# Expert tiles of 128 rows in place of 256, six weight buffers, and a semaphore for each weight matrix

## The chip, the core and the metric

The kernel runs on one core of one Trainium2 chip. The metric is the time of one execution on the device, in microseconds (us). The core has five engines that run side by side and wait for each other through semaphores: TensorE (PE: matrix products into the accumulation memory PSUM; PEld is its stream of weight loads), VectorE (DVE), ScalarE (ACT), GpSimd (POOL) and SyncE (SP). SP and POOL issue the DMAs; 16 DMA engines carry them out.

## What is computed

Two blocks of a gated cross-attention model over x (8 x 512 rows of 256). The change touches only the last step, a layer of eight experts, of which each of the 4096 rows uses one:

```
logits = x_flat @ w_gate + b_gate
route_idx = argmax(softmax(logits))            # one expert of 8 for each row
route_p = max(softmax(logits))
h = relu(x_flat @ W1[e] + b1[e])               # W1[e]: 256 x 1024
y = h @ W2[e] + b2[e]                          # W2[e]: 1024 x 256
x = x + tanh(g_ffn[1]) * y[route_idx] * route_p
```

Everything is float32. One expert's two matrices hold 1 MiB each.

## The kernel before

For some 2940 us the kernel works through the eight batch elements: three attention layers, whose units are interleaved on the engines by tables of numbers (`U_...`), and at the end of each element a normalised row, a residual row and the row's gate weight are stored to DRAM (`dramR`, 528 floats for each row). None of that is touched by the change, apart from two constant ramps.

Then comes the expert stage. The rows are sorted by expert on the device: VectorE ranks them, counts the rows of each expert and splits each expert's rows into tiles of TS = 256 rows. Since the number of rows of an expert is not known when the program is built, ET = 4096 / 256 + 7 = 23 tiles always run; `tex[j]` holds tile j's expert, and `idg` the row numbers that tile j gathers, in pieces of 128 (NH = 2 pieces for a tile). For each tile j:

- SP, `load_weights(j)` (L511 to L523), reads the expert's number and issues four DMAs: W1, b1, W2 and b2 (b2 repeated for 128 partitions). There are two buffers, and one semaphore for each buffer, `w_loaded[par]`, that counts all four. Tile j waits for `v_y`, VectorE's count of finished pieces, to show tile j-2 done.
- POOL, `fetch(j)` (L677), gathers NH pieces of 128 rows from `dramR` into `xs`, XB = 3 tiles ahead; `give_back(j)` (L686) scatters the results to `dramO`.
- TensorE: `turn_rows(j)` (L1326) turns the tile's rows with KD x NH = 4 transposes; `hidden(j)` (L1338) makes 8 x 2 products with a 128x128 block of W1 as the weights and the TS turned rows as the moving columns; `outputs(j)` (L1349) makes, for each of NH pieces, 8 products with 128 rows of `hT` as the weights and 256 columns of W2 moving. A float32 product is two instructions in the trace, so hidden and outputs have 32 each for a tile. The order is hidden(j), turn_rows(j+1), outputs(j).
- ScalarE, `hidden(j)` (L877), applies bias and relu, 8 operations of 128 x TS for a tile, from PSUM to `hT`.
- VectorE, `rows_in(j)` (L1813), copies the turned rows to SBUF; `rows_out(j)` (L1817) adds b2, scales and adds the residual, two operations for a piece.

After the last piece has been scattered, SP copies `dramO` to the output in eight DMAs (L533).

Of the kernel before, what the change touches and what calls it, by code (L numbers as in the profile page):

```python
# [8 lines left out]
F32 = mybir.dt.float32  # L9
# [3 lines left out]
ALU = mybir.AluOpType  # L13
# [3 lines left out]
B, S, C, D = 8, 512, 1601, 256  # L17
P = 128
QT = S // P
KD = D // P  # L20
# [22 lines left out]
NE, FF = 8, 1024  # L43
FM = FF // P
TOK = B * S
NT = TOK // P
TS = 256
ET = TOK // TS + NE - 1
NH = TS // P
NJ = ET * NH  # L50
TE = NT - QT
RW = 2 * D + 16
XB = 3
MASKED = -float(2.0 ** 100)

MB, F0, F1, F2, SB, VB = (0, 1), 2, 3, 4, (5, 6), 7
# [32 lines left out]

HBK = FM * TS // 512  # L90


def h_place(j, m):

    return 2 + (HBK * j + m // (FM // HBK)) % 4, m % (FM // HBK) * TS

# [38 lines left out]
def past(engine, signal, n):  # L135
    if not isinstance(n, int) or n > 0:
        engine.wait_ge(signal, n)


def flamingo(nc, a):  # L140
    ctx_stack = ExitStack()
    with ctx_stack:
        def sem(name):
            return ctx_stack.enter_context(nc.semaphore(name))
# [4 lines left out]
        PS = ctx_stack.enter_context(nc.psum_tensor("PS", [P, 8, 512], F32))  # L149
# [50 lines left out]
        def carve(region, size):  # L200
            at = [0]

            def take(dims, dt, parts=P):
                n = int(np.prod(dims)) * (4 if dt in (F32, I32, U32) else 2)
                words = -(-n // 4)
                ap = region[0:parts, at[0]:at[0] + words]
                at[0] += words
                assert at[0] <= size, (at[0], size)
                if dt is not F32:
                    ap = ap.bitcast(dt)  # L210
                if dt in (BF16,) and words * 2 != int(np.prod(dims)):
                    ap = ap[:, 0:int(np.prod(dims))]
                names = "abcd"[:len(dims)]
                if len(dims) > 1:
                    ap = ap.rearrange(f"p ({' '.join(names)}) -> p {' '.join(names)}",
                                      **{k: v for k, v in zip(names, dims)})
                return ap
            return take
# [5 lines left out]
        take = carve(regAB, R_AB)  # L224
# [4 lines left out]
        take = carve(regAB, R_AB)  # L229
# [9 lines left out]
        take = carve(regC, R - R_AB)  # L239
# [24 lines left out]
        take = carve(regAB, R_AB)  # L264
# [11 lines left out]
        ncount = take([NE], F32)  # L276
        cmp = take([NE, TOK // TS], F32)
        below = take([NE, NE], F32)
# [8 lines left out]
        iota_e = take([NE], F32)  # L287
        iota_k = take([TOK // TS], F32)
        iota_q = take([NT - 1], F32)
# [6 lines left out]
        take = carve(regC, R - R_AB)  # L296
        hT = take([FM, TS], F32)
        ys = [take([NH, D], F32) for _ in range(2)]
        w1 = [take([KD, FF], F32) for _ in range(2)]
        w2 = [take([FM, D], F32) for _ in range(2)]  # L300
        b1 = [take([FM], F32) for _ in range(2)]
        b2 = [take([D], F32) for _ in range(2)]
        xs = [take([NH, RW], F32) for _ in range(XB)]
        xsT = [take([KD, TS], F32) for _ in range(2)]

# [41 lines left out]

        g_late, v_oh, pe_rank, v_tex, v_ohr, v_oht, pe_id, v_id = (
            sem(n) for n in ("g_late", "v_oh", "pe_rank", "v_tex", "v_ohr", "v_oht", "pe_id", "v_id"))
        w_loaded = [sem(f"w_loaded{i}") for i in range(2)]  # L350
        xs_loaded = [sem(f"xs_loaded{i}") for i in range(XB)]
        pe_xsT, v_xsT, pe_h, a_h, pe_y, v_y = (sem(n) for n in ("pe_xsT", "v_xsT", "pe_h", "a_h", "pe_y", "v_y"))
        ys_stored = [sem(f"ys_stored{i}") for i in range(2)]
# [8 lines left out]
        def _(sp):  # L362
# [146 lines left out]
                                         ).then_inc(ld["ones"], 16)  # L509

            def load_weights(j):  # L511
                par = j % 2
                if j >= 2:
                    sp.wait_ge(v_y, NH * (j - 1))
                e = sp.value_load(tex[0:1, j:j + 1], min_val=0, max_val=NE - 1)
                sp.dma_start(w1[par], a["D_W1"][bass.ds(e, 1)].rearrange("o (k p) f -> p (o k) f", p=P)
                             ).then_inc(w_loaded[par], 16)
                sp.dma_start(b1[par], a["D_b1"][bass.ds(e, 1)].rearrange("o p m -> (o p) m")
                             ).then_inc(w_loaded[par], 16)
                sp.dma_start(w2[par], a["D_W2"][bass.ds(e, 1)].rearrange("o (k p) n -> p (o k) n", p=P)  # L520
                             ).then_inc(w_loaded[par], 16)
                sp.dma_start(b2[par], a["D_b2"][bass.ds(e, 1)].rearrange("o n -> (o n)").partition_broadcast(P)
                             ).then_inc(w_loaded[par], 16)  # L523

            sp.wait_ge(n_stored, 16 * B)
            sp.wait_ge(x_stored, 16 * B)
# [1 line left out]
            for j in range(ET):  # L528
                load_weights(j)
# [8 lines left out]
        def _(pool):  # L538
# [138 lines left out]
            def fetch(j):  # L677
                if j >= XB:
                    pool.wait_ge(v_y, NH * (j - XB + 1))
                for t in range(NH):  # L680
                    c = NH * j + t
                    pool.indirect_dma_start(out=xs[j % XB][:, t, :], out_offset=None, in_=dramR,
                                            in_offset=IndirectOffsetOnAxis(ap=idg[:, c:c + 1], axis=0)
                                            ).then_inc(xs_loaded[j % XB], 16)

# [22 lines left out]
        def _(act):  # L708
# [166 lines left out]
                        start_next(b + 2, u)  # L875

            def hidden(j):  # L877
                par = j % 2
                act.wait_ge(w_loaded[par], 64 * (j // 2 + 1))
                for m in range(FM):  # L880
                    bank, at = h_place(j, m)
                    act.wait_ge(pe_h, HBK * j + m // (FM // HBK) + 1)
                    act.activation(hT[:, m, :], PS[:, bank, at:at + TS], ACT.Relu,  # L883
                                   bias=b1[par][:, m:m + 1]).then_inc(a_h, 1)

            for j in range(ET):
                hidden(j)
# [3 lines left out]
        def _(pe):  # L891
            mm, tr = nc.tensor.matmul, nc.tensor.transpose
            FB = (F0, F1)
            pe.wait_ge(ld["a"], 16)
            for m in range(KD):
                for k in range(KD):
                    last = mm(PS[:, m, 0:D], qgA[:, k, m * P:(m + 1) * P], qgA[:, k, D:2 * D],
                              start=k == 0, stop=k == KD - 1)
# [409 lines left out]
            for t in range(QT):  # L1308
                pe.wait_ge(v_oh, 2)
                for i in range(t + 1):  # L1310
                    last = mm(PS[:, 0, t * NE:(t + 1) * NE], lt if i == t else onesD, oh[:, TE + i, :],
                              start=i == 0, stop=i == t)
            for i in range(QT):
                last = mm(PS[:, 0, QT * NE:(QT + 1) * NE], onesD, oh[:, TE + i, :], start=i == 0, stop=i == QT - 1)
            last.then_inc(pe_rank, 1)
            for i in range(NT):
# [4 lines left out]
                for k in range(2):  # L1321
                    last = mm(PS[:, 1, 0:NJ], ohr[k][:, i, :], oht[:, i, :], start=i == 0 and k == 0,
                              stop=i == NT - 1 and k == 1)
# [12 lines left out]
                last.then_inc(pe_xsT, 1)  # L1336

            def hidden(j):  # L1338
                pe.wait_ge(w_loaded[j % 2], 64 * (j // 2 + 1))
                pe.wait_ge(v_xsT, j + 1)  # L1340
                for m in range(FM):
                    bank, at = h_place(j, m)
                    for kk in range(KD):
                        last = mm(PS[:, bank, at:at + TS], w1[j % 2][:, kk, m * P:(m + 1) * P], xsT[j % 2][:, kk, :],  # L1344
                                  start=kk == 0, stop=kk == KD - 1)
                    if (m + 1) % (FM // HBK) == 0:
                        last.then_inc(pe_h, 1)

            def outputs(j):  # L1349
                for t in range(NH):  # L1350
                    past(pe, v_y, NH * j + t - 1)
                    for m in range(FM):
                        if t == 0:
                            pe.wait_ge(a_h, FM * j + m + 1)
                        last = mm(PS[:, 6 + (NH * j + t) % 2, 0:D], hT[:, m, t * P:(t + 1) * P], w2[j % 2][:, m, :],  # L1355
                                  start=m == 0, stop=m == FM - 1)
                    last.then_inc(pe_y, 1)

# [9 lines left out]
        def _(dve):  # L1368
            own = Ticks(v_self)
            v = nc.vector  # L1370
# [320 lines left out]
            def alone(ins):  # L1691
                ins.then_inc(*own.tick())
                dve.wait_ge(v_self, own.now())
# [45 lines left out]
            for b in range(-2, B + 1):  # L1739
                for u in range(NU):  # L1740
                    g, w = u // UN, u % UN
# [75 lines left out]
            def rows_out(j):  # L1817
                par = j % 2
                past(dve, ys_stored[par], 16 * NH * (j // 2))
                for t in range(NH):  # L1820
                    dve.wait_ge(pe_y, NH * j + t + 1)
                    alone(v.tensor_tensor(ys[par][:, t, :], PS[:, 6 + (NH * j + t) % 2, 0:D], b2[par], ALU.add))
                    v.scalar_tensor_tensor(out=ys[par][:, t, :], in0=ys[par][:, t, :],
                                           scalar=xs[j % XB][:, t, 2 * D:2 * D + 1], in1=xs[j % XB][:, t, D:2 * D],
                                           op0=ALU.mult, op1=ALU.add).then_inc(v_y, 1)
# [64 lines left out]
```

## Time and profile before

| | |
|---|---|
| median of 3 runs | 3290.82 us (3289.27 to 3303.54) |
| the profiled execution | 3308.77 us, of which 3307.0 us is the span from first to last instruction |
| PE busy | 2877.2 us (87%) |
| DVE, ACT, POOL busy | 1719.2, 1459.8, 316.6 us |
| attention and sorting | 0 to about 2956 us of the span |
| expert tiles on TensorE | 2956.2 to about 3287.3 us |
| last scatter and output copy | to 3307.0 us |

The profile gives busy times of the engines, the chain of work that ended last, instructions in order of time, and for any stretch the granted TensorE clock (1.00 is 2.4 GHz, 0.50 is 1.2 GHz), the mean busy share of the 16 DMA engines and what they moved. The share is summed from the times of the packets and can come out somewhat over 1.00.

### The profile page before, as it was taken

What the parts mean: (1) busy time and instruction counts of PE and PEld (TensorE: products, weight loads), DVE (VectorE), ACT (ScalarE), POOL (GpSimd) and SP (SyncE); (2) the same over time, 40 slices, a digit from 0 to 9 for tenths busy, and PEclk for the clock granted to TensorE, in tenths of its full rate; (3) what the DMA queues carried; (4) which work ended last, traced back from release to release, by engine and by line L of the source; (5) the groups of instructions that cost most, each with busy time, mean ns of one, the idle gap of its engine ahead of it and who ended that gap; (6) DMA issues with size and microseconds to landing.
All of it is one profiled execution on the core that took longest, in us unless ns stands there. A gap on an engine that the chain in (4) does not pass through costs nothing.

```text
span 3307.0 us, 38212 instructions
## 1 busy us (share of the span) xinstructions
PE 2877.2 (87%) x13236; PEld 1331.4 (40%) x13236; DVE 1719.2 (52%) x4156; ACT 1459.8 (44%) x2794; POOL 316.6 (10%) x364
## 2 busy tenths in 40 slices
PE   5758988998899888998899889988998888859997
PEld 3423423353334333443344334433343322148886
DVE  1335556556555656555655565555555676621111
ACT  2122454545454555445454545454545555612221
POOL 0110001010100100010101010101010000012221
PEclk7878998999899999999999999998999999969999
DMA  4124212322232214220323032303221121026665
GB/s 156 54 70 110 56 34 77 88 61 50 70 94 55 64 36 119 55 74 28 99 69 80 16 119 62 82 20 119 63 63 33 53 55 36 8 90 220 219 208 175
DMA packets 190687, 267.58 MB, mean 81 GB/s; under 512 B 47813, under 2 KB 159661, under 8 KB 190358
## 3 DMA queue, kind: packets, MB, share of 16 engines
q1 hardware_dynamic: 173084, 189.97, 21.3%
q0 software_dynamic: 17408, 75.13, 6.7%
q8 instruction: 107, 1.75, 0.2%
q14 instruction: 88, 0.72, 0.1%
HBM read 203.24 MB, written 65.61 MB: 81 GB/s over the span
## 4 chain that ended last, share of the span: by engine, by line
PE 72%; DVE 15%; ACT 5%; issue 4%; SPq 3%; DMA 1%; POOL 0%; ACTq 0%; POOLq 0%; DVEq 0%
PE PS L1233 12%; PE PS L1184 10%; DVE mxC L1655 9%; PE PS L1216 7%; PE PS L953 6%; PE PS L929 5%; PE PS L1344 5%; PE PS L1355 5%; PE PS L1019 2%; PE PS L1099 2%; PE PS L1036 2%; PE PS L1029 2%; PE PS L976 2%; DVE nmB L1494 1%; PE PS L940 1%
## 5 line engine op out<-in xcount | busy, mean ns | idle before, releaser
L860 ACT ACTIVATE reg<-PS 128x512 f32<-128x512 f32 (+1 forms) x1664 | 970.3, 598 | 1205.2 <-PE PS L1216 1201.9
L1655 DVE TENSOR_REDUCE mxC<-PS 128x1 f32<-128x400 f32 (+1 forms) x2048 | 1090.1, 569 | 752.9 <-PE PS L1184 743.2
L1184 PE MATMUL PS<-reg 96*128 96x400 bf16 (+1 forms) x2048 | 693.0, 351 | 176.5 <-DVE mxC L1655 155.7
L1216 PE MATMUL PS<-reg 99*128 99x512 bf16 (+1 forms) x1664 | 642.5, 396 | 32.5 <-ACT reg L860 27.1
L1184 PEld LDWEIGHTS PS<-reg 96*128 96x128 bf16 x2048 | 203.1, 99 | 725.0 <-DVE mxC L1655 598.9
L1233 PE MATMUL PS<-reg 128*17 128x512 f32 (+1 forms) x3328 | 461.8, 628 | 0.0
L1216 PEld LDWEIGHTS PS<-reg 99*128 99x128 bf16 (+1 forms) x1664 | 165.6, 102 | 348.5 <-ACT reg L860 159.1
L929 PE MATMUL PS<-reg 128*128 128x512 f32 (+1 forms) x512 | 206.0, 526 | 1.2 <-ACT reg L756 0.7
L883 ACT ACTIVATE reg<-PS,reg 128x256 f32<-128x256 f32 x184 | 77.3, 471 | 271.0 <-PE PS L1344 271.0
L953 PE MATMUL PS<-reg 128*128 128x512 f32 (+1 forms) x416 | 193.1, 598 | 0.4 <-ACT reg L728 0.4
L1344 PE MATMUL PS<-reg 128*128 128x256 f32 x736 | 165.4, 382 | 0.9 <-DVE reg L1815 0.9
L1355 PE MATMUL PS<-reg 128*128 128x256 f32 x736 | 163.3, 379 | 0.0
L1344 PEld LDWEIGHTS PS<-reg 128*128 128x128 f32 x736 | 140.6, 191 | 22.1 <-issue 1.2
L1355 PEld LDWEIGHTS PS<-reg 128*128 128x128 f32 x736 | 137.5, 189 | 19.1
L1029 PE MATMUL PS<-ident,reg 128*128 128x128 f32 x512 | 93.6, 312 | 52.0 <-ACT reg L751 52.0
L929 PEld LDWEIGHTS PS<-reg 128*128 128x128 f32 x512 | 89.6, 195 | 77.5 <-issue 65.6
L559 POOL DMA_DIRECT2D reg<-in_A_mask x32 | 17.9, 562 | 1028.0 <-PE PS L1036 638.5
L1029 PEld LDWEIGHTS PS<-ident,reg 128*128 128x128 f32 x512 | 65.2, 158 | 124.0 <-issue 116.8
L1424 DVE CUSTOM_DVE_ANT_0 reg<-PS,reg 128x512 f32<-128x512 f32 (+1 forms) x128 | 72.4, 568 | 74.0 <-PE PS L929 68.9
L976 PE MATMUL PS<-reg,wkC 128*128 128x400 f32 (+1 forms) x256 | 107.3, 546 | 0.7 <-DVE reg L1486 0.7
L953 PEld LDWEIGHTS PS<-reg 128*128 128x128 f32 (+1 forms) x416 | 78.1, 192 | 73.4 <-issue 67.1
L1494 DVE TENSOR_REDUCE nmB<-PS 128x1 f32<-128x512 f32 x128 | 82.0, 682 | 45.9 <-PE PS L1019 45.9
(202 smaller groups left out, 2614.7 us busy)
## 6 DMA issues: line engine op xcount, KB each, us to landing
reg<-in_D_W SPq DMA_DIRECT2D x46, 1024.0 KB, 7.5
reg<-in_A_mask POOLq DMA_DIRECT2D x32, 800.5 KB, 4.8
dramK<-reg SPq DMA_DIRECT2D x144, 100.0 KB
dramV<-reg SPq DMA_DIRECT2D x48, 272.0 KB, 2.1
reg<-in_ctxT POOLq DMA_DIRECT2D x8, 1601.0 KB, 8.3
reg<-in_ctx POOLq DMA_DIRECT2D x8, 1536.0 KB, 8.1
dramQ<-reg SPq DMA_DIRECT2D x96, 128.0 KB
reg<-dramQ SPq DMA_DIRECT2D x32, 384.0 KB, 5.8
```

The source lines that it names most:

```text
L860: act.activation(pr[u % RING][0:r, :], PS[0:r, s_bank(g, v), :], ACT.Exp).then_inc(a_expC, 1)
L929: last = mm(PS[:, FB[i % 2], 0:w], qgA[:, k, t * P:(t + 1) * P], ctxT[:, k, c0:c0 + w], start=k == 0, stop=k == KD - 1)
L953: last = mm(PS[:, FB[m], :], ctxN[0:r, c, m * P:(m + 1) * P], ptA[0:r, c, :], start=c == 0, stop=c == CT - 1)
L976: last = mm(PS[:, FB[u % 2], 0:w], wkC[:, k, m * P:(m + 1) * P], ctxT[:, k, c0:c0 + w], start=k == 0, stop=k == KD - 1)
L1029: last = tr(PS[:, F2, k * P:(k + 1) * P], pB[i % 4][:, k * P:(k + 1) * P], ident[:])
L1184: last = mm(PS[:, bank, 0:w], qs[(NG * bb + g) % 3][0:ROWS, h, t * P:(t + 1) * P], ks[g % 2][0:ROWS, h, c0:c0 + w], start=True, stop=True)
L1216: last = mm(PS[0:r, bank, :], ks[g % 2][0:STK, h, c * P:c * P + r], qs[(NG * b + g) % 3][0:STK, h, :], start=True, stop=not with_mask)
L1233: last = mm(PS[32 * h:32 * h + DC + 1, VB, :], vc[0:r, c, g * GH + h, :], pr[(UN * g + GH * c + h) % RING][0:r, :], start=c == 0, stop=c = ...
L1344: last = mm(PS[:, bank, at:at + TS], w1[j % 2][:, kk, m * P:(m + 1) * P], xsT[j % 2][:, kk, :], start=kk == 0, stop=kk == KD - 1)
L1355: last = mm(PS[:, 6 + (NH * j + t) % 2, 0:D], hT[:, m, t * P:(t + 1) * P], w2[j % 2][:, m, :], start=m == 0, stop=m == FM - 1)
L1494: v.tensor_reduce(nmB[:, i:i + 1], PS[:, (F0, F1)[h], :], AX.X, ALU.max, negate=True).then_inc(v_nmB, 1)
L1655: v.tensor_reduce(mxC[:, h, t, j:j + 1], PS[:, MB[i % 2], 0:M_CH[j][1]], AX.X, ALU.max).then_inc(v_mx, 1)
```

## The change

TS becomes 128, so a tile is one piece (NH = 1), ET = 4096 / 128 + 7 = 39 tiles run, and NJ, the number of pieces, falls from 46 to 39. The weights get WB = 6 buffers, the gathered rows XB = 4 tiles (of one piece each). W1 and b1 have one semaphore for each buffer, W2 and b2 another; `hidden` waits for the first, `outputs` and `rows_out` for the second. Tile j's loads wait for tile j-6 to be done, and those of tile 2 for the gather of tile 1. PSUM holds the hidden products of a tile in HBK = 2 banks in place of 4 (`h_place` still goes round four banks).

```diff
-TS = 256
+TS = 128
 ET = TOK // TS + NE - 1
 NH = TS // P
-XB = 3
+XB = 4
+WB = 6
@@
-        w1 = [take([KD, FF], F32) for _ in range(2)]
-        w2 = [take([FM, D], F32) for _ in range(2)]
-        b1 = [take([FM], F32) for _ in range(2)]
-        b2 = [take([D], F32) for _ in range(2)]
+        w1 = [take([KD, FF], F32) for _ in range(WB)]
+        w2 = [take([FM, D], F32) for _ in range(WB)]
+        b1 = [take([FM], F32) for _ in range(WB)]
+        b2 = [take([D], F32) for _ in range(WB)]
@@
-        w_loaded = [sem(f"w_loaded{i}") for i in range(2)]
+        w1_loaded, w2_loaded = ([sem(f"w{k}_loaded{i}") for i in range(WB)] for k in (1, 2))
@@
             def load_weights(j):
-                par = j % 2
-                if j >= 2:
-                    sp.wait_ge(v_y, NH * (j - 1))
+                par = j % WB
+                if j >= WB:
+                    sp.wait_ge(v_y, NH * (j - WB + 1))
+                if j == 2:
+                    sp.wait_ge(xs_loaded[1], 16 * NH)
...
-                             ).then_inc(w_loaded[par], 16)
+                             ).then_inc(w1_loaded[par], 16)
...
-                             ).then_inc(w_loaded[par], 16)
+                             ).then_inc(w2_loaded[par], 16)
@@ ScalarE
             def hidden(j):
-                par = j % 2
-                act.wait_ge(w_loaded[par], 64 * (j // 2 + 1))
+                par = j % WB
+                act.wait_ge(w1_loaded[par], 32 * (j // WB + 1))
@@ TensorE
             def hidden(j):
-                pe.wait_ge(w_loaded[j % 2], 64 * (j // 2 + 1))
+                pe.wait_ge(w1_loaded[j % WB], 32 * (j // WB + 1))
...
             def outputs(j):
+                pe.wait_ge(w2_loaded[j % WB], 32 * (j // WB + 1))
@@ VectorE
             def rows_out(j):
                 par = j % 2
                 past(dve, ys_stored[par], 16 * NH * (j // 2))
+                dve.wait_ge(w2_loaded[j % WB], 32 * (j // WB + 1))
```

TensorE, the first tiles of the expert stage, before (L1344 hidden, L1334 turn_rows, L1355 outputs; each row's operand is out 128 x columns):

```order
L1344 MATMUL PS<-reg 128x256 [waits v_xsT,w_loaded0]
L1344 MATMUL PS<-reg 128x256 x15
L1334 MATMUL PS<-ident,reg 128x128 [waits v_id,xs_loaded1]
L1334 MATMUL PS<-ident,reg 128x128 x3
L1355 MATMUL PS<-reg 128x256 [waits a_h] x8
L1355 MATMUL PS<-reg 128x256 x8
```

The same place after (L1347 hidden, L1337 turn_rows, L1359 outputs):

```order
L1347 MATMUL PS<-reg 128x128 [waits v_xsT,w1_loaded0]
L1347 MATMUL PS<-reg 128x128 x15
L1337 MATMUL PS<-ident,reg 128x128 [waits v_id,xs_loaded1]
L1337 MATMUL PS<-ident,reg 128x128
L1359 MATMUL PS<-reg 128x256 [waits a_h,w2_loaded0]
L1359 MATMUL PS<-reg 128x256 [waits a_h] x7
```

A tile keeps its 16 hidden products at half the columns, has half of the transposes and half of the output products, and the outputs wait for W2 by themselves.

SP, between the weights of tile 1 and those of tile 2, before:

```order
L522 DMA reg<-in_D_b 128x256
L515 TENSOR_LOAD reg [waits v_y]
L515 ISA x2
L516 ISA
L516 DMA reg<-in_D_W 128x2x1024
```

And after:

```order
L525 DMA reg<-in_D_b 128x256
L518 TENSOR_LOAD reg [waits xs_loaded1]
L518 ISA x2
L519 ISA
L519 DMA reg<-in_D_W 128x2x1024
```

The loads of tiles 2 to 5 now stand behind one wait, for the gather of tile 1, and only from tile 6 on behind `v_y`.

## Rows read from the trace of the kernel before

**Rows 1.** The page: busy tenths, clock and DMA in 40 slices of the span

```profile
PE   5758988998899888998899889988998888859997
PEclk7878998999899999999999999998999999969999
DMA  4124212322232214220323032303221121026665
GB/s 156 54 70 110 56 34 77 88 61 50 70 94 55 64 36 119 55 74 28 99 69 80 16 119 62 82 20 119 63 63 33 53 55 36 8 90 220 219 208 175
```

**Rows 2.** Chain that ended last, expert stage: start us, us, what

```profile
2947.84 6.37 DMA reg<-dramR,reg
...
2956.24 9.21 PE PS L1344 x32
2965.88 6.94 PE PS L1355 x32
2972.82 6.93 PE PS L1344 x32
2980.19 6.94 PE PS L1355 x32
2987.13 6.93 PE PS L1344 x32
...
3280.30 3.48 PE PS L1355 x16
```

**Rows 3.** Instructions by line, 2930 to 3307: busy us, mean ns | idle before, releaser

```profile
L883 ACT ACTIVATE reg<-PS,reg 128x256 f32<-128x256 f32 x184 | 77.3, 471 | 271.0 <-PE PS L1344 271.0
L692 POOL DMA_INDIRECT dramO<-reg x46 | 45.5, 989 | 239.0 <-DVE reg L1823 239.0
```

**Rows 4.** TensorE in order of time, from one tile to the next: start us, us, what

```profile
2993.90 0.60 PE L1334 MATMUL PS<-ident,reg 128*128 128x128 f32 x4
2994.33 7.10 PE L1355 MATMUL PS<-reg 128*128 128x256 f32 x32
3001.27 7.09 PE L1344 MATMUL PS<-reg 128*128 128x256 f32 x32
```

**Rows 5.** TensorE, short float32 products in the attention stage: start us, us, what

```profile
724.40 1.85 PE L1087 MATMUL PS<-wgD,reg 128*128 128x8 f32 x16
...
1636.78 0.56 PE L929 MATMUL PS<-reg 128*128 128x65 f32 x4
1637.17 0.38 PE L1216 MATMUL PS<-reg 99*128 99x512 bf16 x1
```

**Rows 6.** Stretches: from:to, us, busy (x), clock, DMA share, GB/s

```profile
2940.00:2942.50 2.50, 1.26 (x33) 1.13 (x30) 2.25 (x12) 0.00 (x0) 0.00 (x0) 0.50 0.95 383
2945.75:2946.75 1.00, 0.00 (x0) 0.00 (x0) 0.41 (x2) 0.00 (x0) 0.32 (x1) 0.50 0.43 82
2946.75:2956.75 10.00, 1.62 (x5) 1.21 (x6) 0.69 (x1) 0.00 (x0) 5.53 (x6) 0.50 1.05 380
2939.75:2956.75 17.00, 3.63 (x53) 2.96 (x51) 6.11 (x25) 0.00 (x0) 5.84 (x6) 0.50 0.99 351
3060.14:3074.44 14.30, 14.30 (x70) 12.49 (x69) 2.51 (x5) 3.36 (x8) 3.92 (x5) 1.00 0.63 212
3246.11:3260.42 14.31, 14.31 (x70) 12.50 (x69) 2.51 (x5) 3.36 (x8) 3.82 (x5) 1.00 0.68 212
```

**Rows 7.** DMA queues from 2974 to 2989: MB, share of 16 engines over 15 us

```profile
q1 hardware_dynamic: 1600, 2.23, 47.0%
q0 software_dynamic: 256, 0.80, 14.0%
```

**Rows 8.** Start of the stage: SP, POOL and PE in order of time

```profile
2938.25 0.40 SPq L516 DMA_DIRECT2D reg<-in_D_W  x1
...
2942.70 4.67 SPq L522 DMA_DIRECT2D reg<-in_D_b  x1
...
2946.43 1.10 POOL L682 DMA_INDIRECT reg<-dramR,reg  x1 [23.53 <-DVE reg L1810]
...
2954.25 1.11 PE L1334 MATMUL PS<-ident,reg 128*128 128x128 f32 x4 [9.01 <-DMA reg<-dramR,reg]
```

More of the change, by code:

```diff
@@ L511, in load_weights @@
             def load_weights(j):
-                par = j % 2
-                if j >= 2:
-                    sp.wait_ge(v_y, NH * (j - 1))
+                par = j % WB
[3 more added lines that the diff above has]
+                    sp.wait_ge(xs_loaded[1], 16 * NH)
                 e = sp.value_load(tex[0:1, j:j + 1], min_val=0, max_val=NE - 1)
                 sp.dma_start(w1[par], a["D_W1"][bass.ds(e, 1)].rearrange("o (k p) f -> p (o k) f", p=P)
-                             ).then_inc(w_loaded[par], 16)
+                             ).then_inc(w1_loaded[par], 16)
                 sp.dma_start(b1[par], a["D_b1"][bass.ds(e, 1)].rearrange("o p m -> (o p) m")
-                             ).then_inc(w_loaded[par], 16)
+                             ).then_inc(w1_loaded[par], 16)
                 sp.dma_start(w2[par], a["D_W2"][bass.ds(e, 1)].rearrange("o (k p) n -> p (o k) n", p=P)
-                             ).then_inc(w_loaded[par], 16)
+                             ).then_inc(w2_loaded[par], 16)
                 sp.dma_start(b2[par], a["D_b2"][bass.ds(e, 1)].rearrange("o n -> (o n)").partition_broadcast(P)
-                             ).then_inc(w_loaded[par], 16)
+                             ).then_inc(w2_loaded[par], 16)
             sp.wait_ge(n_stored, 16 * B)
@@ L1343, in hidden @@
                     for kk in range(KD):
-                        last = mm(PS[:, bank, at:at + TS], w1[j % 2][:, kk, m * P:(m + 1) * P], xsT[j % 2][:, kk, :],
+                        last = mm(PS[:, bank, at:at + TS], w1[j % WB][:, kk, m * P:(m + 1) * P], xsT[j % 2][:, kk, :],
                                   start=kk == 0, stop=kk == KD - 1)
@@ L1354, in outputs @@
                             pe.wait_ge(a_h, FM * j + m + 1)
-                        last = mm(PS[:, 6 + (NH * j + t) % 2, 0:D], hT[:, m, t * P:(t + 1) * P], w2[j % 2][:, m, :],
+                        last = mm(PS[:, 6 + (NH * j + t) % 2, 0:D], hT[:, m, t * P:(t + 1) * P], w2[j % WB][:, m, :],
                                   start=m == 0, stop=m == FM - 1)
@@ L1819, in rows_out @@
                 past(dve, ys_stored[par], 16 * NH * (j // 2))
+                dve.wait_ge(w2_loaded[j % WB], 32 * (j // WB + 1))
                 for t in range(NH):
                     dve.wait_ge(pe_y, NH * j + t + 1)
-                    alone(v.tensor_tensor(ys[par][:, t, :], PS[:, 6 + (NH * j + t) % 2, 0:D], b2[par], ALU.add))
+                    alone(v.tensor_tensor(ys[par][:, t, :], PS[:, 6 + (NH * j + t) % 2, 0:D], b2[j % WB], ALU.add))
                     v.scalar_tensor_tensor(out=ys[par][:, t, :], in0=ys[par][:, t, :],
```

## Prediction

> **What bounds the kernel now.** I read first the slices of the page [rows 1]: the last four and a half slices are the expert stage, where TensorE is busy to nine tenths, the DMA engines only to six, and the clock is at its upper level. The change works there alone. Then the chain that ended last [rows 2]: from 2956.24 on it is TensorE and nothing else, hidden (L1344) and outputs (L1355) in turn, until 3280.30 + 3.48 = 3283.8; the second half of the last tile's outputs takes another 3.48 and ends at 3287.3. A tile is one hidden, one outputs and the transposes between: 2987.13 - 2972.82 = 14.31 us. The first hidden takes 9.21 us where the others take 6.93, since TensorE starts cold: 2.3 us. So 23 tiles make the stage. ScalarE and POOL wait for TensorE [rows 3]: 271 us of idle time before ScalarE's relu, 239 us before the scatters. The DMA engines are at 0.63 to 0.68 [rows 6]. TensorE bounds the stage; the next resource is the DMA engines, and this change asks more of them.
>
> **TensorE's part.** A float32 product of 256 columns is two instructions of 6.93/32 = 217 ns each [rows 2], in hidden and outputs alike. The four transposes add 14.31 - 13.87 = 0.44 us, so 0.11 us each. In the changed kernel a tile has:
> - outputs: 16 instructions of 256 columns, 16 x 0.217 = 3.47 us;
> - transposes: two, 0.22 us;
> - hidden: 32 instructions of 128 columns. Such a product is not in the trace. Streaming alone would be half of 217, about 108 ns. The weights of 128x128 have to be loaded for each of them as before, and now there is only half as long a product to hide the load. The load by itself stands in [rows 5]: 16 instructions of 8 columns take 1.85 us; less the last one's own tail of some 0.2 us that is about 107 ns for each, and so short a product cannot be what takes it. Four instructions of 65 columns start 0.39 us before the next operation starts, about 98 ns each, though streaming them would take 55 ns: load and stream run side by side and do not add up to 162. The lower bound for 128 columns is so 107 ns (both alike, wholly beside each other), the upper bound 107 + 108 = 215 ns (one after the other). I take 110 ns, since both short forms of [rows 5] sit on the load alone. Hidden is then 3.52 us.
>
> A tile is 3.47 + 0.22 + 3.52 = 7.21 us, and 39 tiles are 281.2 us against 23 x 14.31 = 329.1 us: **47.9 us less**. The reason is that 39 x 128 = 4992 padded rows replace 23 x 256 = 5888. The cold start costs the same 2.3 us: at half the clock hidden's instructions take twice as long over the same time.
>
> The Trainium skill speaks against this gain. "TensorE: Matmul & The Clock Gate", section "Part 3: Packing small matmuls — row/col tiling", says that a weight load overlaps a running product only when the two use different row groups; these use all rows. The trace does not agree [rows 4]: with loads of about 107 ns laid in series a 256-column instruction would take 320 ns, and 32 of them take 7.10 us. The same page, section "Back-to-back issue gap", gives about 81 ns in a sustained stream for 128 columns against about 56 ns for an isolated one; no row here shows that for float32, and scaled by that ratio the 110 ns would be near 157 ns and the tile some 8.7 us. I keep it as a rival below, with a price of its own from the rows.
>
> **ScalarE, VectorE, POOL.** ScalarE is busy for 3.36 us of a tile now with eight operations of 256 columns [rows 6]; eight of 128 columns cost at most that, in a tile of 7.2, and the first four run beside the second half of hidden, the last four beside transposes and the first four products of outputs (0.22 + 4 x 0.43 = 1.9 us for the first of them to be ready). VectorE has 2.51 us of work for a tile now, POOL 3.92 [rows 6]; both halve, one scatter and one gather of about 1 us each on POOL [rows 3, 8]. The added wait of VectorE for W2 and b2 holds only rows_out, for which TensorE has had to wait for the same semaphore before. All this at nothing, under TensorE's 7.2 us. If TensorE waited, they would have more room still.
>
> **The DMA part.** For each tile the kernel loads W1 and W2 (2.10 MB) and b2 (0.13 MB), gathers 0.27 MB and scatters 0.13 MB. So a tile moves 2.63 MB, in 7.2 us and no longer in 14.3: 365 GB/s where now it is 212 [rows 6] (now two gathers and two scatters, 3.04 MB). Three rows price it:
> - 380 GB/s in the ten saturated us while tile 1's weights and six gathers ran [rows 6]: 6.9 us for a tile.
> - 351 GB/s over the 17 us in which two tiles' weights and the gathers ran, with a dip to 82 GB/s for one us between tile 0's last load and tile 1's first [rows 6]: 7.5 us for a tile.
> - The share of engine time: over 15 us the weights took 47.0% = 7.05 us of all 16 engines and the rows' traffic 14.0% = 2.1 us [rows 7], half of which stays: 8.1 us. Saturated, the view reads 1.05 [rows 6], so 7.7 us; 8.1 if it does not.
> I take 7.5 us, since that stretch is what will now happen all the time: whole tiles of weights queued behind each other and gathers between them. The dip costs less later, when gathers and scatters can fill it. The Trainium skill's "DMA: Bandwidth & Descriptors", section "Measured (HBM→SBUF, 128 partitions, SWDGE, issued from GpSimd)", has 341 GB/s for 1 MB and 425 for 16 MB; by its figures a tile would be 7.7 or 6.2 us, on either side of TensorE's 7.2, so it does not decide.
>
> Now the two in time. **Start:** the tables grow a little (32 counts for each expert in place of 16, 39 tiles in place of 23), three or four short VectorE operations some 0.13 us longer each, less a narrower one-hot: I take +0.3 us for the first gather. It is issued at 2946.7 and lands after 6.7 us or so (the second took 6.37, [rows 2]), and TensorE need not wait for a second piece (the transposes start at 2954.25 now, [rows 8]). Transposes, copy and hidden start by 2954.8, 1.4 us earlier than 2956.24. **TensorE path:** 2954.8 + 2.3 + 281.2 - 0.2 (no transposes in the last tile) = 3238.1. **DMA path:** tiles 0 and 1 as now. SP then waits for tile 1's gather, about 2954.5; first bytes some 1.7 us later (L516 issued at 2938.25 [rows 8], full rate from 2940 [rows 6]), 2956.2. Tile j's W2 and b2 are in at 2956.2 + 7.5 x (j - 1), tile 38's at 3233.7, and its outputs end 3.5 us later, at 3237.2. The six buffers let the loads run ahead, but at 7.5 us against 7.2 the lead is largest at tile 2 (outputs start at 2960.8 + 7.2 x 2, W2 is there at 2956.2 + 7.5: 11.5 us) and is nearly used up at the last tile (1.1 us). SP's blocked issue (4.67 us, [rows 8]) holds up nothing but SP's next loads. The paths meet: I take 3239.5, a little over both because gathers and loads will not arrive evenly. TensorE ends now at 3287.3: **-48 us**. The tail (VectorE, scatter, output copy, 3307.0 - 3287.3 = 19.7 us) is the same. On the profiled 3308.8 us that makes 3261; on the median, which is 18 us lower, 3290.8 - 48 = 3243. I state **3244**, one above, for the small cost of two paths that meet.
>
> **Rivals.**
> - *The DMA engines bound the stage clearly* (7.7 to 8.6 us for a tile). By 7.7 the end is 2956.2 + 37 x 7.7 + 3.5 = 3244.6, -43 us, 3248; by 8.1 it is 3259.4, -28 us, 3263; by 8.6 (every tile pays the dip of 1.1 us on top of 7.5) 3277.9, -9 us, 3281. For it: share 8.1 us [rows 7], the dip. Against: the 380 GB/s while gathers were mixed in.
> - *Slower: the weight load is not hidden under 128 columns.* By the sum above it breaks even at a tile of (3287.3 - 2956.9)/39 = 8.47 us, hidden instructions of (8.47 - 3.69)/32 = 149 ns. Half hidden, 160 ns, gives 39 x 8.81 = 343.6, +13 us, 3304. Wholly in series, 215 ns, gives 39 x 10.57 = 412, +82 us, 3373. Against it: the 65-column products at 98 ns [rows 5].
> - *Slower: DMA engines that lose the dip and more in each tile*, beyond 8.96 us for a tile (where 2956.2 + 37 T + 3.5 = 3287.3); at 9.5 us, +24 us, 3315. It would need 277 GB/s, and only the stretch that follows a pause is that slow.
> - *It does not do what it says*: another engine would have to hold a tile at 7.2 us or over, and the busiest of them has 3.9 us of work in a tile of twice the rows [rows 6]. No chance of its own.
>
> **How the numbers follow.** Forecast (TensorE and DMA within 0.4 us of each other, 3236 to 3250): 0.54. DMA bound, 3250 to 3274: 0.23; 3274 to 3291: 0.07. Load partly hidden, within 16 us of no change: 0.05; clearly slower for it: 0.07. DMA clearly slower: 0.04. A measurement of this kernel can tell about 0.5%, 16 us, from no change. Faster by more is 0.54 + 0.23 = 0.77, within it 0.07 + 0.05 = 0.12, slower 0.07 + 0.04 = 0.11. The range takes 107 ns and 7.0 us for a tile below (39 x 7.12 gives 3234.5, -53 us, 3238, and 2 us for the start) and the dip in most tiles above: 3236 to 3282; what lies above it, near 0.17, are the slower cases and part of those within 16 us.
>
> **What would show it.** Right: hidden (now L1347) at 3.4 to 3.6 us for 32 instructions; outputs 3.47; a tile period of 7.2 to 7.6 us; DMA share above 0.95 and 345 to 370 GB/s; small waits of TensorE for W1 or W2 that appear towards the end of the stage; start of hidden near 2954.8. DMA rival: waits for in_D_W or in_D_b from the first tiles on, period as the share says. Load rival: a busy TensorE without waits and hidden well over 3.6 us. Wrong altogether if the clock falls in the stage because TensorE waits, which at 0.3 us in 7.5 I don't expect.

## The result and the profile after

The changed kernel takes 3252.79 us (median of 4 runs, 3247.28 to 3257.44) against 3292.14 us for the kernel before (4 runs). The ratio is 0.9873 with a 95% interval of 0.9845 to 0.9902: 32 to 51 us faster. The forecast was -48 us, 3244 us. A second measurement with more runs (below) gave 0.984, 0.9819 to 0.9861.

The page of the changed kernel, as in [rows 1]: busy tenths, clock and DMA in 40 slices of a span of 3245.5 us.

```profile
PE   5758988998899988998899889988998888867997
PEclk9877999999989999999999999999999998988999
DMA  4124112222132203230422123122312022009996
GB/s 159 55 63 120 48 37 86 82 62 58 58 99 56 75 29 101 70 81 16 121 63 73 31 86 88 56 51 74 94 49 65 12 74 59 16 14 338 375 375 233
```

Only the last four slices differ clearly: the DMA engines, at six tenths before, now stand at nine tenths for three of them (375 GB/s in two), and TensorE is still busy to nine tenths in the two slices that lie wholly inside the stage. The chain that ended last says which of the two bounds, to be set beside [rows 2]:

```profile
2932.31 6.91 DMA reg<-dramR,reg
2939.27 0.70 PE PS L1337 x2
2939.99 0.44 DVE reg L1819
2940.57 6.43 PE PS L1347 x32
2947.00 0.22 PE PS L1337 x2
2947.22 3.47 PE PS L1359 x16
2950.69 3.57 PE PS L1347 x32
2954.26 0.22 PE PS L1337 x2
2954.48 3.47 PE PS L1359 x16
...
3212.05 3.57 PE PS L1347 x32
3215.62 0.22 PE PS L1337 x2
3215.84 3.48 PE PS L1359 x16
```

It is TensorE alone: hidden 3.57, transposes 0.22, outputs 3.47, 7.26 us for a tile, from the second tile to the last, without one wait for a weight. The instructions by line from 2920 to 3246 (busy us, mean ns, idle time before and what ended it):

```profile
L1347 PE MATMUL PS<-reg 128*128 128x128 f32 x1248 | 148.3, 277 | 0.6 <-DVE reg L1819 0.6
L1359 PE MATMUL PS<-reg 128*128 128x256 f32 x624 | 141.8, 379 | 0.0
L886 ACT ACTIVATE reg<-PS,reg 128x128 f32<-128x128 f32 x312 | 89.3, 369 | 216.3 <-PE PS L1347 216.3
```

TensorE's two lines have 0.6 us of idle time between them, for the first tile's copy. (The mean of 277 ns for one instruction is more than the 111.6 ns from one start to the next, 3.57/32, since instructions overlap; periods are the ones to count with.) ScalarE, with 369 ns for an operation of 128 columns (471 for 256, [rows 3]), waits for TensorE as before, 216.3 us in all.

The stage in stretches (from:to, us, busy time of PE, PEld, DVE, ACT, POOL, then clock, DMA share, GB/s), to be set beside [rows 6]:

```profile
2932.00:2933.00 1.00, 0.00 (x0) 0.00 (x0) 0.06 (x1) 0.00 (x0) 0.69 (x1) 0.50 0.35 86
2949.00:2950.00 1.00, 1.00 (x6) 0.88 (x5) 0.00 (x0) 0.00 (x0) 0.00 (x0) 1.00 0.63 101
2960.00:3190.00 230.00, 230.00 (x1582) 215.90 (x1581) 41.82 (x94) 73.07 (x256) 62.08 (x64) 1.00 1.06 375
3190.00:3210.00 20.00, 20.00 (x144) 18.89 (x143) 4.01 (x9) 6.86 (x24) 4.91 (x5) 1.00 0.69 236
```

For 230 us TensorE is busy all the time and so are the DMA engines. But the loads are done around 3203, 23 us before TensorE's last product at 3226.4: the DMA engines were full because six buffers let them run ahead, and they ran ahead because a tile costs them less than TensorE (e8 below measures by how much). The two dips (86 and 101 GB/s) look like the dip of [rows 6]: in both, as there, POOL's queue moved no packet (in the first, POOL was only issuing the first gather). A third, 130 GB/s from 2942 to 2943, stands where SP's loads begin again after the wait for tile 1's gather (W1 issued at 2941.30). From 2960 to 3199 no stretch of one microsecond moves less than 318 GB/s.

Since the attention part before the stage is long and its length differs between executions, the gain is best read from a mark inside the execution. From the last marking of experts on VectorE (the start of L1697, now L1701, at 2933.89 before, 2919.51 after) to the end of the span it is 373.1 us before and 326.0 us after: **-47.1 us**.

### The profile page after: what moved, and what is told of

It is laid out like the page before. It is cut to its first block, busy times and chain, and to the rows that moved or that the text cites. A ratio compares the mean times of both kernels' runs of the same rounds, so it can differ in the third digit from the quotient of the medians.

```text
span 3245.5 us, 39407 instructions
## 1 busy us (share of the span) xinstructions
PE 2817.1 (87%) x13622; PEld 1304.6 (40%) x13622; DVE 1713.5 (53%) x4158; ACT 1471.2 (45%) x2922; POOL 303.1 (9%) x350
## 4 chain that ended last, share of the span: by engine, by line
PE 71%; DVE 15%; ACT 5%; issue 4%; SPq 3%; DMA 1%; POOL 0%; ACTq 0%; POOLq 0%; DVEq 0%
PE PS L1236 12%; PE PS L1187 10%; DVE mxC L1659 9%; PE PS L1219 7%; PE PS L956 6%; PE PS L932 5%; PE PS L1347 4%; PE PS L1359 4%; PE PS L1022 2%; PE PS L1102 2%; PE PS L1039 2%; PE PS L1032 2%; PE PS L979 2%; DVE nmB L1498 1%; PE PS L943 1%
## 5 line engine op out<-in xcount | busy, mean ns | idle before, releaser
L886 ACT ACTIVATE reg<-PS,reg 128x128 f32<-128x128 f32 x312 | 89.3, 369 | 216.3 <-PE PS L1347 216.3
L1347 PEld LDWEIGHTS PS<-reg 128*128 128x128 f32 x1248 | 147.9, 194 | 3.1 <-issue 1.0
L1347 PE MATMUL PS<-reg 128*128 128x128 f32 x1248 | 148.3, 277 | 0.6 <-DVE reg L1819 0.6
L1359 PE MATMUL PS<-reg 128*128 128x256 f32 x624 | 141.8, 379 | 0.0
L1359 PEld LDWEIGHTS PS<-reg 128*128 128x128 f32 x624 | 115.1, 189 | 15.1
L932 PEld LDWEIGHTS PS<-reg 128*128 128x128 f32 x512 | 89.2, 194 | 77.0 <-issue 65.0
```

The lines of the kernel that those rows point to most:

```text
L932: last = mm(PS[:, FB[i % 2], 0:w], qgA[:, k, t * P:(t + 1) * P], ctxT[:, k, c0:c0 + w], start=k == 0, stop=k == KD - 1)
L1347: last = mm(PS[:, bank, at:at + TS], w1[j % WB][:, kk, m * P:(m + 1) * P], xsT[j % 2][:, kk, :], start=kk == 0, stop=kk == KD - 1)
```

## The experiments

For each profile: "stage" is the time from the first hidden product to TensorE's last one, "tile" the stage over the number of tiles. Each ratio is taken against runs of the kernel before that were made together with it (7 to 18 runs, medians of 3293.9 to 3299.5 us; 4 runs in the row "changed"). e7, e8 and e10 leave out part of the computation, so their times (one run each) are no times of this kernel; they serve to find what a part costs.

| kernel | tiles, buffers | stage, us | tile, us | median, ratio to before [95%] |
|---|---|---|---|---|
| before | 23 x 256, 2 | 331.0 | 14.4 | 3292.1 |
| changed | 39 x 128, 6 | 285.8 | 7.33 | 3252.8, 0.987 [0.985, 0.990] |
| e1 | the same | 285.7 | 7.33 | 3244.7, 0.984 [0.982, 0.986] |
| e2 | 39 x 128, 2 | 321.8 | 8.25 | 3283.9, 0.995 [0.994, 0.997] |
| e3 | 39 x 128, 3 | 285.7 | 7.33 | 3255.2, 0.987 [0.985, 0.990] |
| e4 | 23 x 256, 6 | 330.7 | 14.4 | 3296.4, 1.000 [0.998, 1.001] |
| e5 | 39 x 128, 2, one semaphore | 419.2 | 10.75 | 3380.8, 1.027 [1.025, 1.029] |
| e6 | 39 x 128, 6, one semaphore | 285.8 | 7.33 | 3255.4, 0.987 [0.984, 0.990] |
| e7 | as changed, 64 columns in hidden | 285.7 | 7.33 | 3256.9, one run |
| e8 | as changed, half of the outputs | 267.1 | 6.85 | 3226.7, one run |
| e9 | as e3, TensorE kept warm | 283.2 | 7.26 | 3247.2, 0.986 [0.983, 0.988] |
| e10 | as e8, hardly any biases | 252.4 | 6.47 | 3223.3, one run |

**e1, the changed kernel again.** No edit.

> The changed kernel again, for a tighter ratio. My theory: the gain lies wholly in the expert stage, which in the two profiles went from 350.8 us (first hidden to end of span) to 304.9 us; with an unchanged attention part that is -46 us, a ratio of 0.986. Rival: the attention part is also changed (about +6 us, as the medians 3292.14 and 3252.79 taken alone would have it), then the gain stays at -39 us and the attention part before the first hidden is longer than before's in this profile too, by some 6 us.

Measured: ratio 0.984 [0.9819, 0.9861] against 18 runs of before, 3244.68 us. The stage is the same to 0.1 us (285.7), and from the mark on VectorE (2927.77) to the end of the span (3254.7) it is 326.9 us. The first hidden product started at 2948.82, eight us later than in the first profile of the same program. Over the profiles of this study that start lies between 2933.7 (e3) and 2956.2 (before), with e4, tiles of 256, at 2940.7 and e6, tiles of 128, at 2953.5. So nothing points to a changed attention part; its length varies by more than 10 us from one execution to the next, which is enough for two medians of one program to lie 8 us apart. The theory's -46 us, a ratio of 0.986, is inside both intervals, though at the upper edge of the second. The rival wanted the first hidden some 6 us later than before's 2956.24; it is earlier in both profiles, and the rival falls.

**e2 to e4, the parts of the change alone.**

```diff
 e2:  WB = 6  ->  WB = 2
 e3:  WB = 6  ->  WB = 3
 e4:  TS = 128 -> TS = 256,  XB = 4 -> XB = 3   (WB = 6 stays)
```

> Tiles of 128 rows, but two weight buffers (WB = 2), one semaphore for each matrix. Theory: with two buffers the loads of tile j+2 start only when tile j is done; by the rows of before W2 and b2 are there some 9 us after their issue, 12.2 us after TensorE's end of tile j, and outputs(j+2) can end 3.5 us after that, so two tiles take 15.7 us or more: 7.85 us for a tile in place of 7.26, at least +23 us over the changed kernel, up to 8.9 us (+64 us) if two tiles' loads slow each other. TensorE should wait for W2 or b2 before L1359. Rival: small tiles alone bring the gain, two buffers are enough, no difference to the changed kernel (7.26 us for a tile).

> WB = 3. Theory: three tiles' time (21.8 us) is longer than the 15.7 us from one tile's end to the third-next tile's end, so TensorE does not wait and a tile takes 7.26 us: no difference to the changed kernel. Rival: since the DMA engines need 7.0 us for a tile of 7.26, a pause in loading cannot be made up, and three buffers lose some us in all (tile period 7.3 to 7.6, +2 to +13 us).

> The other part alone: TS = 256 with six buffers and the split semaphores (XB = 3). Theory: in the kernel before TensorE never waited for a weight, so nothing is gained, a tile stays at 14.31 us and the time is that of before within 0.3%. Rival: buffers and semaphores bring some of the gain; then 5 us or more faster than before.

e2: 8.25 us for a tile, stage +36 us over the changed kernel, inside the expected +23 to +64. The waits of TensorE in e2 (engine, line, waited for: us in total, times, longest):

```profile
PEld PS L1347 <- DMA reg<-in_D_b: 26.5, 29, 1.8
PE PS L1347 <- DMA reg<-in_D_b: 14.9, 21, 1.4
PEld PS L1359 <- DMA reg<-in_D_b: 12.4, 12, 1.5
PE PS L1359 <- DMA reg<-in_D_b: 9.5, 10, 1.3
```

TensorE waits for the bias, the last load of each pair, ahead of hidden (L1347) 21 times and ahead of outputs (L1359) 10 times. I had expected it at the outputs alone, and had left out that W1 and b1 are late too: for one pair of tiles, b1 is issued 2.6 us after TensorE's end of tile j (3071.8 and 3074.32) and lands 6.0 us after its issue (median of the stage), 8.6 us where hidden(j+2) could start after 7.3. These waits are short, and the granted clock stays at 1.00 from 2950 to 3240. With small tiles and two buffers 0.5% is left of a gain of 1.3 to 1.6%.

e3: no wait at all, 285.7 us. Three buffers do what six do. SP is now held by VectorE's count before it may load, 36 times:

```profile
SPq L518 <- DVE reg L1828: 77.9, 36, 8.5
```

These 77.9 us are no idle time of the DMA engines, which still work on the loads issued before. Over 230 us of this stage (same columns as the stretches above):

```profile
2950.00:3180.00 230.00, 230.00 (x1591) 216.13 (x1591) 42.39 (x96) 72.39 (x254) 62.66 (x64) 1.00 1.05 362
```

The share reads 1.05 here too, at 362 GB/s, which is TensorE's pace (2.63 MB in 7.26 us): a full share does not say that the engines could move no more. The rival (a pause cannot be made up) falls.

e4: 1.000 [0.998, 1.001], 14.3 us for a tile as before. Buffers and semaphores without the smaller tiles bring nothing, since TensorE never waited for a weight [rows 2]; e2 has shown that the smaller tiles need them.

**e5 and e6, one semaphore for all four loads.** e5 has two buffers, e6 six. In both, `w1_loaded` and `w2_loaded` become one `w_loaded` with a count of 64 for a tile, for which hidden waits on TensorE and on ScalarE; the waits in outputs and rows_out go.

```diff
-                pe.wait_ge(w1_loaded[j % WB], 32 * (j // WB + 1))
+                pe.wait_ge(w_loaded[j % WB], 64 * (j // WB + 1))
...
-                pe.wait_ge(w2_loaded[j % WB], 32 * (j // WB + 1))
```

> Tiles of 128 rows, two buffers, one semaphore for all four loads of a tile, as in the kernel before: the tile size alone. Theory: hidden(j+2) cannot start before W2 and b2 are there, 12.2 us after the end of tile j, so two tiles take 12.2 + 7.26 = 19.5 us, 9.7 us for a tile, +95 us over the changed kernel: slower than before by about 50 us. Rival: the semaphore makes no difference (as e2).

> Six buffers with one semaphore for each buffer. Theory: the loads run ahead of TensorE by more than a tile at all times, so it does not matter that hidden waits for W2 as well: tile period 7.26 us, no difference to the changed kernel. At most some us at tiles 2 and 3, whose loads are issued late. Rival: the split semaphores matter, TensorE waits for W2 before hidden in many tiles, +10 us or more.

e6 is the changed kernel to 0.1 us: with six buffers the second semaphore is worth nothing. e5 is slower than before by 2.7%, and by 133 us in the stage where I had expected 95. The direction and the place are right, the size is not, and the order in time shows why (TensorE; start us, us; in brackets the idle time before and what ended it):

```profile
3066.27 5.28 PE L1347 MATMUL PS<-reg 128*128 128x128 f32 x32 [5.48 <-DMA reg<-in_D_b]
3071.39 0.38 PE L1337 MATMUL PS<-ident,reg 128*128 128x128 f32 x2
3071.61 3.63 PE L1358 MATMUL PS<-reg 128*128 128x256 f32 x16
3075.08 3.73 PE L1347 MATMUL PS<-reg 128*128 128x128 f32 x32
```

And in stretches:

```profile
3060.80:3066.20 5.40, 0.00 (x0) 0.00 (x0) 0.91 (x2) 0.00 (x0) 1.96 (x2) 0.97 1.07 368
3066.20:3071.40 5.20, 5.13 (x33) 5.13 (x34) 0.00 (x0) 1.14 (x4) 0.00 (x0) 0.70 1.05 358
3071.40:3075.10 3.70, 3.70 (x21) 3.26 (x20) 0.43 (x1) 1.14 (x4) 0.00 (x0) 1.00 0.07 21
```

Every second tile TensorE stands idle for some 5 us (19 waits, 92.0 us in all, where the expectation's sum of waits was 95), and then works part of the next hidden at the lower clock (mean 0.70): 5.28 us in place of 3.73. Over the stage hidden's busy time is 186.6 us where the changed kernel has 148.3. That is 38 us which the wait costs after it has ended, and just the part of the 133 us that my sum of waits had left out.

**e7, what sets the pace of hidden.** The products take 64 of the tile's 128 rows; the rest of each tile's hidden values is left out.

```diff
-  mm(PS[:, bank, at:at + TS], w1[...], xsT[j % 2][:, kk, :], ...)
+  mm(PS[:, bank, at:at + 64], w1[...], xsT[j % 2][:, kk, 0:64], ...)
```

> Hidden products with 64 of the 128 moving columns (half of the tile's hidden values are left out). Theory: a 128-column float32 product stands where weight load and streaming are level, so with 64 columns the load alone is left, 107 ns for an instruction in place of 111.6: hidden 3.42 us in place of 3.57, a tile 7.11. Rival: the load is hidden or cheap and streaming sets the pace, then an instruction takes about 56 ns, hidden 1.8 us, and the tile 5.5 us, or what the DMA engines allow (7.0 us).

The chain that ended last in e7:

```profile
2956.85 4.26 PE PS L1359 x16
2961.11 3.52 PE PS L1347 x32
2964.85 3.47 PE PS L1359 x16
2968.32 3.52 PE PS L1347 x32
```

Half of the columns saves 0.05 us of 3.57: an instruction takes 110 ns with 64 columns and 111.6 ns with 128. So the streaming does not set the pace; what is left fits the weight load, which is the same in both. (No run changed the size of the load itself, so another fixed cost of a float32 instruction is not excluded.) The rival (56 ns) falls by a factor of two, and the theory's 107 ns was 3 ns low. The stage is no shorter, for another reason: in this execution TensorE worked slowly for longer at the start, the first hidden took 7.06 us and the first outputs 4.26 (mean clock 0.55 from 2949.3 to 2959.3), which gives back what the later tiles save.

**e8 and e10, what a tile costs the DMA engines.** e8 sums over 4 of 8 blocks in outputs; e10 besides loads b1 and b2 for j < 6 only, with the counts that are waited for lowered to match.

```diff
-                    for m in range(FM):
+                    for m in range(FM // 2):
```

> The outputs sum over 4 of the 8 blocks only (half of the output products are left out; all loads stay). TensorE then needs 7.26 - 1.74 = 5.5 us for a tile, and the DMA engines must become the bound: this measures what a tile costs them. By the trace of the changed kernel, 2.63 MB at 375 GB/s, it is 7.0 us: the stage ends only about 10 us earlier, with the last loads at the same place. By the prediction it was 7.5 us: then the stage would be no shorter than now and the loads would end some 17 us later than in the changed kernel.

> e8 (half of the output products left out), and b1 and b2 loaded for the first six tiles only (later tiles use what lies in the buffer). It prices the two small loads for the DMA engines. Theory: they cost what their bytes cost: 2.50 MB for a tile at 375 GB/s, 6.67 us between two tiles' loads in place of 7.06 in e8. Rival: 128 packets of 32 bytes for b1 and the broadcast of one row for b2 hold the engines for longer than their bytes, as the dip to 82 GB/s between two tiles in the kernel before would have it: 6.3 us or less.

With 5.5 us of work for a tile, TensorE now waits for loads. The largest wait of TensorE's products in e8, and then 60 us of the steady part of e8 and of e10:

```profile
PE PS L1347 <- DMA reg<-in_D_b: 36.2, 31, 2.0
```

```profile
3050.00:3110.00 60.00, 49.60 (x359) 43.97 (x358) 11.60 (x26) 18.26 (x64) 17.18 (x18) 1.00 1.06 374
```

```profile
3050.00:3110.00 60.00, 52.79 (x381) 46.72 (x380) 12.19 (x28) 20.54 (x72) 17.62 (x18) 1.00 1.05 381
```

SP is no longer held by VectorE's count; its issue of b2 lasts up to 5.5 us in e8 and tile follows tile at the pace of the DMA engines. In e8 31 tiles lie between the W1 load issued at 2971.11 and the one at 3189.90: **7.06 us for a tile**. In e10, 29 tiles between 2989.91 and 3182.34: 6.64 us. (The stages of the table, divided by the tiles, are a little lower, since the first tiles' loads are ahead.) So the DMA engines need 7.06 us where TensorE needs 7.26: in the changed kernel they are not the bound, by 3%. My 7.0 for e8 and 6.67 for e10 held; the small loads cost about what their bytes cost (0.13 MB, 0.42 us), and b1's 128 packets of 32 bytes nothing that can be seen in that. The expectation for the length of e8's stage did not hold: it came out 19 us shorter, not 10. The last loads end at the same place as expected (some 263 us after the first hidden starts, in both kernels), but the changed kernel's TensorE ended 23 us after them, and e8's only 4 us after.

**e9, the cold start.**

```diff
+            pe.wait_ge(v_id, 2)
+            for _ in range(9):
+                mm(PS[:, 2, 0:D], ident[:], wvA[:, 0, :], start=True, stop=True)
             turn_rows(0)
```

> Three weight buffers as in e3, and nine float32 products of 256 columns into bank 2, which nobody reads, between the last sorting step and the first gather's landing, while TensorE has nothing to do. Theory: the first hidden takes 6.4 us and not 3.57 because TensorE has stood idle at half the clock; kept busy, it starts it at the upper level: hidden(0) 3.6 us, the stage (first hidden to end of span) 303 us in place of 306. In the median 3 us is below what shows; the time should be that of the changed kernel. Rival: the first hidden waits for something else (weights, ScalarE) and stays at 6.4 us; or the products run past the gather and hold the transposes back by 1 us or more.

TensorE in order of time in e9, and three stretches of the same:

```profile
2931.54 5.95 PE L1365 MATMUL PS<-wvA,ident 128*128 128x256 f32 x18 [0.98 <-DVE reg L1817]
2938.73 0.44 PE L1337 MATMUL PS<-ident,reg 128*128 128x128 f32 x2 [1.25 <-DMA reg<-dramR,reg]
2939.78 3.81 PE L1347 MATMUL PS<-reg 128*128 128x128 f32 x32 [0.61 <-DVE reg L1822]
```

```profile
2931.50:2934.50 3.00, 2.96 (x7) 2.42 (x8) 0.00 (x0) 0.00 (x0) 2.15 (x3) 0.50 0.95 304
2934.50:2938.50 4.00, 2.99 (x12) 2.20 (x11) 0.00 (x0) 0.00 (x0) 1.80 (x2) 0.91 1.07 366
2939.70:2943.50 3.80, 3.72 (x33) 3.75 (x34) 0.00 (x0) 1.15 (x4) 0.00 (x0) 1.00 0.82 264
```

The products that nobody reads raise the clock to its upper level before the rows arrive; the first hidden then takes as long as any other, and stage and tail are 303.0 us, as expected, against 306.1 for the same kernel without them (e3) and 304.9 to 305.9 with six buffers. The median (3247.24) is within the scatter of e1 and e3, so this shows in the trace and not in the time. It is the shortest stage of the kernels that compute everything, with three buffers in place of six.

## Why the prediction was right, and where it was not

- **The sum as a whole.** -48 us was predicted for the stage with its start, -47.1 us is what the two profiles show from the mark on VectorE on. That it is so close is in part luck. TensorE's path alone gave -49.2 us (3238.1 against 3287.3). Hidden then cost 2.0 us more over the 39 tiles and the cold start 0.6 us more; the 1.4 us that were added for two paths that meet had nothing behind them and stood in their place; the tail, taken as the same, was 0.6 us shorter (19.2 against 19.8).
- **The median.** The first median showed -39 us and the second -55, which fits the attention part's scatter (e1). At 3252.8 us the first lies among the times that the prediction had given to a DMA bound (3250 to 3274), but the trace shows no such bound; e1's 3244.7 lies among the forecast's own.
- **Tile arithmetic**: right. 39 x 7.26 in place of 23 x 14.31. e4 shows that nothing else in the change brings time by itself, e2 and e3 that at least three buffers have to go with it.
- **Hidden at 128 columns**: predicted 110 ns, measured 111.6, 7.26 us for a tile and not 7.21, +2 us in all. The upper bound of 215 ns (load after stream) and the rival built on it fell, and so did the 157 ns that the prediction had set beside it. e7 supports the reason: an instruction takes about 107 ns with 8 columns [rows 5], 110 with 64, 111.6 with 128 and 217 with 256, which fits a load of about 110 ns beside a stream that draws level with it at 128 columns. The Trainium skill's "TensorE: Matmul & The Clock Gate", section "Part 3: Packing small matmuls — row/col tiling", says in one sentence that a load overlaps a running product only for other row groups. The same section also lets a load into a background weight buffer run ahead, which is the case that these rows would fit. Taken alone, the first sentence does not agree with them: load and stream, with all 128 rows in use, about 110 and (as half of 217, an estimate) 108 ns, take 111.6 ns together.
- **Outputs, transposes, sorting**: 3.47 and 0.22 us as predicted; the sorting chain grew by 0.24 us (12.11 to 12.35 from the mark to the last index operation) where +0.3 was assumed.
- **Cold start**: mis-sized. 2.3 us was taken as the same as before; the first hidden cost 6.43 - 3.57 = 2.86 us over a warm one. e9 shows it to be the clock, which stood at 0.50 for the first 5.4 us of hidden after the change and for about 4.2 us before it; why for longer is open (in e7 it was some 9 us).
- **The DMA price**: this step failed, without harm. 7.5 us for a tile came from the 351 GB/s of a stretch with a ramp and a dip in it [rows 6]. Measured are 7.06 us (e8) and 375 GB/s. The row that was right was the 380 GB/s with rows and weights mixed. The dip was not seen in the steady part, where POOL has rows to move; that they fill it is what the traces suggest, the cause of the dip itself was not tried. The count by share was too high as well (7.05 us of engine time for the weights of a tile [rows 7]). It had been read in bursts after a pause; that packets which wait for their first bytes count as busy there would explain it, and is not shown. In e8, with the engines never idle, the queues have less for each tile (3000 to 3150: packets, MB, share of 16 engines):

```profile
q1 hardware_dynamic: 34110, 47.42, 90.1%
q0 software_dynamic: 2755, 8.64, 15.5%
```

Over 150 us and 7.06 us for a tile that is 6.4 us for the weights and 1.1 for the rows. So the picture of two paths that meet at the end was wrong: the loads were 23 us ahead at the end and not 1, and the small waits of TensorE towards the end, named as a sign of being right, did not appear. 375 GB/s lies above the 345 to 370 that were named.
- **The slower side.** The case on the other side of no change exists, though for none of the reasons that I had priced: it comes when the buffers do not cover the distance from one tile's end to the next load's landing (e5: +87 us against before).
- **Two slips in the working**, neither of which moved the forecast: the tile time at which the DMA path breaks even is (3287.3 - 2959.7)/37 = 8.85 us and not 8.96; and the 107 ns of [rows 5] come from start to start (1.70 us for 16 instructions), where taking 0.2 us off 1.85 gives 103.

## What to carry to other kernels

Padding to whole tiles is work: with eight experts and a fixed worst case, halving the tile took 15% of the rows away. Here it pays down to 128 columns of float32; with 64 (e7) hidden's products are hardly shorter, so a tile of half the rows would cost TensorE nearly the same, and the load traffic for each row would double again (an estimate; no such tile was run). Count buffers by time: from the end of a tile to the end of the next one in the same buffer, if it waits for nothing but its loads, over one tile's work. Here that is 16.5 us (two tiles of 8.25 in e2) over 7.26, which makes three, and e3 ran as fast as six; beyond that they are only memory.

A wait for loads costs TensorE more than its length: after some 5 us of standing idle a part of the next work ran at the lower clock, 38 us over the stage in e5, while the waits of at most 1.4 us in e2 left the clock at its upper level. And when DMA engines look full, ask whether they are ahead or behind: the share reads 1.06 in the changed kernel and 1.05 in e3, where they bounded nothing, and 1.06 in e8, where they did. The difference shows in who waits, TensorE or nobody.

## What was not expected of the hardware

- The DMA engines had 3% to spare, 7.06 us against 7.26 for a tile. A tile of 128 rows is near both limits at once, TensorE's time for a float32 instruction (111.6 ns, where 110 is the least that 64 columns took) and the DMA engines' rate.
- A float32 product with 64 moving columns takes as long as one with 128: 110 and 111.6 ns.
- In e2 and e5 the load that is waited for is a bias of 4 or 128 KB, not the matrix of 1 MB that is issued just ahead of it in the same queue.
- The DMA engines' busy share stood at 1.05 at 362 GB/s (e3) and at 1.06 at 375 (e8): it does not tell a full queue from one that keeps another engine's pace.
